# Level 0's odd maps: the high part held twice, one column apart, and level 2's stride-2 layer multiplied image by image

## The chip, the core and the metric

The kernel runs on one core of a Trainium2 chip. The metric is the device time of one execution in microseconds, lower is better. All times below are of this one core.

## What is computed

Two images of 32 channels and 64 x 64 pixels are normalised per channel, go through a small residual U-net, and are added to its result:

```python
def basic_block(x, w1, w2, stride=1, ds=None):
    out = jax.nn.relu(conv3(x, w1, stride) * BN_S)
    out = conv3(out, w2, 1) * BN_S
    identity = conv1x1(x, ds, stride) * BN_S if ds is not None else x
    return jax.nn.relu(out + identity)
...
x = basic_block(x, e0b0c1, e0b0c2)                          # level 0: 64 x 64
x = basic_block(x, e0b1c1, e0b1c2)
f0 = x
x = basic_block(x, e1b0c1, e1b0c2, stride=2, ds=e1b0ds)     # level 1: 32 x 32
x = basic_block(x, e1b1c1, e1b1c2)
f1 = x
x = basic_block(x, e2b0c1, e2b0c2, stride=2, ds=e2b0ds)     # level 2: 16 x 16
x = basic_block(x, e2b1c1, e2b1c2)
x = (jax.nn.relu(deconv2(x, dec0w) * BN_S) + f1) * BN_S
x = (jax.nn.relu(deconv2(x, dec1w) * BN_S) + f0) * BN_S
...
x = x + _L0_conv_ref(_gn(x), ...)
```

## The kernel before

**Maps in blocks.** A map of 64 x 64 pixels is kept as 32 x 32 blocks of 2 x 2 pixels: 4 pixels of a block times 32 channels fill the 128 partitions. A 3 x 3 convolution is then a sum over four shifts of a 2 x 2 stencil of blocks, each one product with a 128 x 128 weight. The output of the first convolution of a block pair lies half a block off, in 33 x 33 blocks (an "odd" map); the second convolution reads that map and returns to 32 x 32 ("even"). The four shifts `s` are (sy, sx) with sx = s mod 2.

**High and low parts.** Every operand is kept as an fp32r high part and an fp32r remainder. A piece of output is the sum of three groups of four matmuls: high weight by high map, low weight by high map, high weight by low map, 12 in all, into one PSUM bank.

**Stages and pieces.** The stages of level 0 are e0b0c1 (odd), e0b0c2 (even), e0b1c1 (odd), e0b1c2 (even). An odd stage has, per image, three pieces of 11 rows of 33 (364 columns a matmul, read as one run from the map `flat0`, pitch 33). An even stage has two pieces of 16 rows of 32 (512 columns) per image, read from the odd map `odd0`, laid out at L184 with `ODD0_PITCH` 36: `moving` (L948) takes 16 rows of 32 elements out of rows that are 36 apart. Pieces 0 to 5 are e0b0c1, 6 to 9 e0b0c2, 10 to 15 e0b1c1, 16 to 19 e0b1c2. Then come e1b0c1 (stride 2) and the rest of level 1 with 290 or 272 columns, level 2 with 164 or 144 for both images together, and the two upsampling stages.

**Who does what.** TensorE runs all matmuls in program order; nearly all are recorded on L837, the helper `products`. For an odd piece of level 0, VectorE applies ReLU and mask from the bank to `relu` (L763); ScalarE copies that to the high part (L545) and then prepares the high part of the next weight (`weights_hi`, L504); GpSimd subtracts to get the low part (L470). VectorE makes the low part of a weight (`weights_lo`, L604) after each piece; it needs `weights_hi` of the same weight, which ScalarE issues behind the high part of the piece before. VectorE writes a `relu` slot again only when the low part of four pieces earlier is there (L717). For an even piece VectorE adds the residual into `block0` (L767, L769), ScalarE makes the high part (L545, or L541 in e0b1c2) and VectorE the low part (L798, L793). SyncE loads the raw weights in four slots, each when the low part of the weight four earlier is done (L425).

**Level 2's stride-2 layer (e2b0c1).** Its input is split by pixel into four planes for both images. TensorE takes, for each image as it becomes ready, the five high products (L972, 82 columns); then for both images together five products of the low weights with the high map, five with the low map (L837, 164 columns), and, after waiting for `sides_by_act` and `sides_by_dve`, six with gathered half-width operands ("sides"). VectorE produces image 1's planes (L727, L734) behind its copies of sides for image 0 (L682); ScalarE gathers sides (L517) and, for the 1 x 1 shortcut, corners (L509), in the order sides of image 0, corners of image 0, sides of image 1, one corner of image 1. The next stage, e2b0c2, starts with three shortcut products once all corners are there (`corner_by_dve`, `corner_ready`), two filling matmuls on zeros, and 12 products of 144 columns that wait for e2b0c1's result from VectorE (L763).

**Skips.** ScalarE scales `block0` into `normed` (L554), GpSimd adds the input (L480), ScalarE reorders it into the tensor `skip0` (L578, 16 copies), for the last stage's additions.

Of the kernel before, what the change touches and what calls it, by code (L numbers as in the profile page):

```python
# [27 lines left out]
F32 = mybir.dt.float32  # L28
F32R = mybir.dt.float32r
BF16 = mybir.dt.bfloat16  # L30
ACT = mybir.ActivationFunctionType
ALU = mybir.AluOpType
# [8 lines left out]
ODD0_PITCH = 36  # L41
# [123 lines left out]
def build(nc, x, consts, weights, out):  # L165
    ctx = ExitStack()
    with ctx:  # L167
# [10 lines left out]
        skip0 = sb("skip0", [P, 8, IMAGES, 2, 8, 8])  # L178
# [5 lines left out]
        odd0 = sb("odd0", [P, 2, IMAGES, ODD_ROWS[0], ODD0_PITCH], F32R)  # L184
        flat1 = odd0[:].rearrange("p h i r c -> p (h i r c)")[:, 0:2 * IMAGES * MAP[1]].rearrange(
# [14 lines left out]
        odd = [odd0[:, :, :, :, 0:ODD_COLS[0]], odd1, odd2[:]]  # L200
# [160 lines left out]
        def split_of(piece, half):  # L361

            stage = STAGES[piece.stage]
            if stage.level == 0:
                if stage.kind == "odd":
                    return odd[0][:, half, piece.images[0], piece.row:piece.row + piece.rows, :]
                return flat_inside(half, piece.images, piece.row, piece.rows)
            return odd[stage.level][:, half] if stage.level == 2 else odd[1][:, half, piece.images[0]]
# [11 lines left out]
        def skip0_of(n):  # L380
            return skip0[:, n].rearrange("p i j a b -> p (i j a b)")

# [59 lines left out]
        def _(pool):  # L442
# [24 lines left out]
            for piece in LEVEL0:  # L467
                if STAGES[piece.stage].residual is None:
                    wait_half(pool, piece.index, 0)
                    pool.tensor_tensor(split_of(piece, 1), fp32_of(piece), split_of(piece, 0).bitcast(F32),  # L470
                                       ALU.subtract).then_inc(lo_ready, 1)
# [28 lines left out]
        def _(act):  # L500
# [36 lines left out]
            for piece in LEVEL0:  # L537
                wait_relu(act, piece.index)
                if STAGES[piece.stage].name == "e0b1c2":
                    for i in range(2):  # L540
                        last = act.activation(planes_inside(1, 0, piece.images[0], i, piece.row // 2, piece.rows // 2),  # L541
                                              fp32_of(piece)[:, i::2].rearrange("p r (c b) -> p b r c", b=2), ACT.Relu)
                    last.then_inc(hi_ready, 1)
                else:
                    act.activation(split_of(piece, 0), fp32_of(piece), ACT.Relu).then_inc(hi_ready, 1)  # L545
# [21 lines left out]
            gather_corners(2, 0)  # L567
            gather_sides(2, 1)
            gather_corners(2, 1, range(3, 4))
            for image in range(IMAGES):  # L570
                act.wait_ge(skip0_added, image + 1)
# [261 lines left out]
        def _(pe):  # L833
# [60 lines left out]
            for piece in PIECES[:DEC0[0].index]:  # L894
# [14 lines left out]
                elif level == 0:  # L909
                    target = rows_0(target, piece)  # L910
# [27 lines left out]

                def moving(half, s):
# [7 lines left out]
                    if level == 0:  # L947
                        return odd[0][:, half, images[0], piece.row + sy:piece.row + sy + piece.rows,  # L948
                                      sx:sx + BLOCKS[0]]
# [15 lines left out]
                if stage.kind == "down":  # L965

                    whole = [[moving(half, shifts * sy + sx) for sy, sx in WHOLE] for half in range(2)]
                    if level == 2:
                        for image in images:
                            wait_half(pe, source_of_level(2, image), 0)  # L970
                            for n, m in enumerate(whole[0]):
                                pe.matmul(target[:, image], w[:, 0, n], m[:, image], start=(image == 0 and n == 0),  # L972
                                          stop=False, skip_group_check=True)
                        wait_w_lo(pe, k)
                        products(target, [(w[:, 1, n], m) for n, m in enumerate(whole[0])], first=False, final=False,
                                 skip=True)
# [37 lines left out]
                last = products(target, low_terms, first=False, final=not shortcut_last)  # L1014
# [129 lines left out]
```

## Time and profile before

| | us |
|---|---|
| median of 3 runs | 91.69 (91.61 to 91.88) |
| the profiled execution | 91.54 |
| its span, first to last instruction | 89.7 |
| TensorE (PE) busy, share of the span | 83.0, 92% |
| VectorE (DVE) busy | 63.7, 71% |
| ScalarE (ACT) busy | 44.9, 50% |
| GpSimd (POOL) busy | 27.5, 31% |
| mean granted TensorE clock | 0.982 |

Busy shares say how full an engine is over the whole span, not whether it sets the end; for that one follows the chain of work that ended last, and in a stretch where one engine is on that chain, the distance from the start of one of its instructions to the start of the next. Matmuls overlap, so the duration recorded for one (some 400 ns for 512 columns) is longer than the time it takes in a stream; starts are what counts. PEld is the weight load that goes with each matmul.

### The profile page before, as it was taken

Reading aid. Unit: us, or ns where it says so; the run is one execution under the profiler, and the core shown is the slowest. Engines: PE = TensorE matmul, PEld = TensorE weight load, DVE = VectorE, ACT = ScalarE, POOL = GpSimd, SP = SyncE. Lnnn points to the kernel's source line nnn. Section 1 sums busy time; section 2 is a strip of 40 time slices with the busy share of each in tenths; the row PEclk is TensorE's granted clock in tenths of the full one; section 3 lists DMA queues with packets and bytes.
Section 4 is the critical chain, followed back from the end, with each engine's and each line's share of the span. In section 5 each row is a group of like instructions: output and inputs, shape, how many; then the busy total and the mean of one; then the engine's idle time right before and its main releaser. Section 6 shows DMA issues by size and latency. Waiting matters only on the chain.

```text
span 89.7 us, 1547 instructions
## 1 busy us (share of the span) xinstructions
PE 83.0 (92%) x537; PEld 73.9 (82%) x537; DVE 63.7 (71%) x189; ACT 44.9 (50%) x94; POOL 27.5 (31%) x43
## 2 busy tenths in 40 slices
PE   5988999999999999999999999999999989999900
PEld 3666999998777799999977777999999989887600
DVE  5579999799968799655635569999638797543650
ACT  6007015877435065744423259999910089990410
POOL 7300070999910000654440000300794002400140
PEclk9999999999999999999999999999999999999975
DMA  2989900045673003550000000000000000000075
GB/s 23 255 251 324 323 22 0 7 122 125 154 217 112 4 14 121 168 168 5 0 0 0 0 0 4 0 0 0 7 0 0 4 0 0 7 0 0 0 258 210
DMA packets 4183, 6.51 MB, mean 73 GB/s; under 512 B 464, under 2 KB 2128, under 8 KB 4176
## 3 DMA queue, kind: packets, MB, share of 16 engines
q1 hardware_dynamic: 4032, 6.29, 23.0%
q10 hardware_dynamic: 144, 0.13, 0.4%
q8 instruction: 4, 0.07, 0.3%
q14 instruction: 3, 0.02, 0.1%
HBM read 5.37 MB, written 1.05 MB: 72 GB/s over the span
## 4 chain that ended last, share of the span: by engine, by line
PE 83%; DVE 7%; DMA 3%; issue 1%; ACT 1%; POOLq 1%; DVEq 0%
PE psum L837 78%; DMA x_sb<-x_in 3%; PE psum L876 2%; DVE stats L611 2%; DVE split L727 1%; PE psum L972 1%; POOLq L167 1%; DVE shared L682 1%; PE psum L1029 1%; DVE split L734 1%; PE psum L862 1%; DVE moments L626 1%; DVE shared L640 1%; PE psum L869 1%; ACT result L586 0%
## 5 line engine op out<-in xcount | busy, mean ns | idle before, releaser
L470 POOL TENSOR_TENSOR odd<-relu,odd 128x363 fp32r<-128x363 f32 x12 | 13.4, 1134 | 16.0 <-ACT odd L545 16.0
L837 PE MATMUL psum<-shared,w_e0b0c 128*128 128x364 f32 x72 | 12.5, 332 | 0.4 <-DVE shared L640 0.4
L837 PEld LDWEIGHTS psum<-shared,w_e0b0c 128*128 128x128 f32 x72 | 12.0, 189 | 0.7 <-issue 0.7
L837 PE MATMUL psum<-shared,w_e0b1c 128*128 128x364 f32 x72 | 12.2, 329 | 0.0
L837 PEld LDWEIGHTS psum<-shared,w_e0b1c 128*128 128x128 f32 x72 | 12.1, 188 | 0.1
L837 PE MATMUL psum<-odd,w_e0b1c 128*128 128x512 f32 x48 | 12.0, 411 | 0.0
L837 PE MATMUL psum<-odd,w_e0b0c 128*128 128x512 f32 x48 | 12.0, 411 | 0.0
L763 DVE SCALAR_TENSOR_TENSOR relu<-psum,inside 128x363 f32<-128x363 f32 (+2 forms) x18 | 8.7, 489 | 3.8 <-PE psum L837 3.6
L837 PEld LDWEIGHTS psum<-odd,w_e0b0c 128*128 128x128 f32 x48 | 9.1, 190 | 2.6
L837 PEld LDWEIGHTS psum<-odd,w_e0b1c 128*128 128x128 f32 x48 | 9.1, 190 | 2.6
L545 ACT ACTIVATE odd<-relu 128x363 fp32r<-128x363 f32 x12 | 6.2, 520 | 7.4 <-DVE relu L763 7.4
L869 PE MATMUL psum<-zeros 128*128 128x256 bf16 x42 | 7.2, 330 | 1.1 <-DVE eps L660 1.1
L517 ACT ACTIVATE shared<-split 64x164 fp32r<-64x164 f32 (+2 forms) x7 | 3.1, 440 | 7.5 <-DVE split L734 6.5
L480 POOL TENSOR_TENSOR normed<-normed,x_sb 128x1024 f32<-128x1024 f32 x2 | 4.8, 2408 | 6.4 <-DVE shared L782 6.4
L869 PEld LDWEIGHTS psum<-zeros 128*128 128x128 bf16 x42 | 4.6, 119 | 2.4 <-DVE eps L660 1.1
L463 POOL TENSOR_TENSOR shared<-normed,shared 128x352 fp32r<-128x352 f32 (+1 forms) x4 | 3.2, 819 | 10.9 <-DVE normed L620 10.9
L545 ACT ACTIVATE shared<-block 128x512 fp32r<-128x512 f32 x4 | 2.5, 636 | 6.7 <-DVE block L767 6.7
L541 ACT ACTIVATE split<-block 128x256 fp32r<-128x256 f32 x8 | 3.0, 427 | 4.9 <-DVE block L769 4.8
L509 ACT ACTIVATE shared<-split 32x544 fp32r<-32x544 f32 x8 | 5.2, 656 | 0.1
L578 ACT ACTIVATE skip<-normed 128x128 f32<-128x128 f32 x16 | 5.2, 421 | 0.0
L837 PE MATMUL psum<-shared,w_e1b0c 128*128 128x272 f32 (+1 forms) x36 | 5.2, 292 | 0.0
L769 DVE SCALAR_TENSOR_TENSOR block<-block,psum 128x512 f32<-128x512 f32 x4 | 2.8, 689 | 3.0 <-PE psum L837 2.9
(126 smaller groups left out, 140.4 us busy)
## 6 DMA issues: line engine op xcount, KB each, us to landing
x_sb<-x_in SPq DMA_DIRECT2D x4, 160.0 KB, 3.9
raw<-e0b0c_in SPq DMA_DIRECT2D x2, 256.0 KB, 4.7
raw<-e0b1c_in SPq DMA_DIRECT2D x2, 256.0 KB, 4.9
raw<-e1b1c_in SPq DMA_DIRECT2D x2, 256.0 KB, 3.2
raw<-e2b1c_in SPq DMA_DIRECT2D x2, 256.0 KB, 2.6
raw<-e1b0c_in SPq DMA_DIRECT2D x1, 448.0 KB, 3.6
raw<-e2b0c_in SPq DMA_DIRECT2D x1, 448.0 KB, 4.1
x_sb<-x_in SPq DMA_DIRECT2D x2, 192.0 KB, 3.9
```

What stands on the lines that cost most here:

```text
L463: pool.tensor_tensor(flat_inside(1, [image], row, rows), normed[:, image, row:row + rows, :], flat_inside(0, [image], row, rows).bitcast(F32),
L470: pool.tensor_tensor(split_of(piece, 1), fp32_of(piece), split_of(piece, 0).bitcast(F32), ALU.subtract).then_inc(lo_ready, 1)
L480: pool.tensor_tensor(normed[:, image], normed[:, image], x_sb[:, image], ALU.add).then_inc(skip0_added, 1)
L509: last = act.activation(*corner_copy(level, image, q), ACT.Copy)
L517: last = act.activation(target, source, ACT.Copy)
L541: last = act.activation(planes_inside(1, 0, piece.images[0], i, piece.row // 2, piece.rows // 2), fp32_of(piece)[:, i::2].rearrange("p r ( ...
L545: act.activation(split_of(piece, 0), fp32_of(piece), ACT.Relu).then_inc(hi_ready, 1)
L578: last = act.activation(target, source, ACT.Copy)
L763: last = dve.scalar_tensor_tensor(out=target, in0=sums, scalar=0.0, in1=mask, op0=ALU.max, op1=ALU.mult)
L769: last = dve.scalar_tensor_tensor(out=target, in0=block0[:, image, rows, :], scalar=0.0, in1=sums, op0=ALU.max, op1=ALU.add)
L837: last = pe.matmul(target, w, moving, start=(first and n == 0), stop=(final and n == len(terms) - 1), skip_group_check=skip)
L869: pe.matmul(psum[:, bank, 0:256], zeros[:, 0:P], zeros[:, 0:256], start=True, stop=True)
```

## The change

The odd map of level 0 is split in two tensors. `odd0_hi` has no padding: rows of 32, and for each image two versions, version sx holding columns sx to sx + 31 of the 33. A shift's 16 rows are then one run of 512 elements. `odd0_lo` holds the low part once, with rows of 33 (before: 36), so its reads are still 16 rows of 32. ScalarE writes both versions (two activations of 32 columns a row where there was one of 33), and GpSimd subtracts in two steps, 32 columns against version 0 and the last column against version 1. `skip0` has no memory of its own any more and lies in `block0`, with a wait on ScalarE ahead of the first write. At level 2 the five low-weight products of e2b0c1 are made image by image, right behind the high ones, and ScalarE's corner copies of image 0 are split around its side copies of image 1.

```diff
 FLAT = (BLOCKS[0] + 2) * FLAT_PITCH + 2
-ODD0_PITCH = 36
 PITCH = [b + 1 for b in BLOCKS]
...
         block0 = sb("block0", [P, IMAGES, 32, 32])
-        skip0 = sb("skip0", [P, 8, IMAGES, 2, 8, 8])
+        skip0 = block0[:].rearrange("p i r c -> p (i r c)").rearrange("p (n i j a b) -> p n i j a b", n=8, i=IMAGES,
+                                                                     j=2, a=8)
         skip1 = sb("skip1", [P, 2, 2, 2, IMAGES, 8, 8], F32R)
...
         planes = [None, split0, split1]
-        odd0 = sb("odd0", [P, 2, IMAGES, ODD_ROWS[0], ODD0_PITCH], F32R)
-        flat1 = odd0[:].rearrange("p h i r c -> p (h i r c)")[:, 0:2 * IMAGES * MAP[1]].rearrange(
+        odd0_hi = sb("odd0_hi", [P, IMAGES, 2, ODD_ROWS[0], BLOCKS[0]], F32R)
+        odd0_lo = sb("odd0_lo", [P, IMAGES, ODD_ROWS[0], ODD_COLS[0]], F32R)
+        flat1 = odd0_hi[:].rearrange("p i v r c -> p (i v r c)")[:, 0:2 * IMAGES * MAP[1]].rearrange(
             "p (h i n) -> p h i n", h=2, i=IMAGES)
...
             "p (h i n) -> p h i n", h=2, i=IMAGES)
-        odd = [odd0[:, :, :, :, 0:ODD_COLS[0]], odd1, odd2[:]]
+        odd = [None, odd1, odd2[:]]
         corner = [None, corner1, corner2[:]]
...
             if stage.level == 0:
-                if stage.kind == "odd":
-                    return odd[0][:, half, piece.images[0], piece.row:piece.row + piece.rows, :]
                 return flat_inside(half, piece.images, piece.row, piece.rows)
...
             return skip0[:, n].rearrange("p i j a b -> p (i j a b)")
+
+        def high_shifted(piece, shift):
+            return odd0_hi[:, piece.images[0], shift, piece.row:piece.row + piece.rows, :]
+
+        def low_rows(piece):
+            return odd0_lo[:, piece.images[0], piece.row:piece.row + piece.rows, :]

...
                     wait_half(pool, piece.index, 0)
-                    pool.tensor_tensor(split_of(piece, 1), fp32_of(piece), split_of(piece, 0).bitcast(F32),
+                    last_column = slice(BLOCKS[0], ODD_COLS[0])
+                    pool.tensor_tensor(low_rows(piece)[:, :, 0:BLOCKS[0]], fp32_of(piece)[:, :, 0:BLOCKS[0]],
+                                       high_shifted(piece, 0).bitcast(F32), ALU.subtract)
+                    pool.tensor_tensor(low_rows(piece)[:, :, last_column], fp32_of(piece)[:, :, last_column],
+                                       high_shifted(piece, 1)[:, :, BLOCKS[0] - 1:].bitcast(F32),
                                        ALU.subtract).then_inc(lo_ready, 1)
...
                     last.then_inc(hi_ready, 1)
+                elif STAGES[piece.stage].kind == "odd":
+                    for shift in range(2):
+                        last = act.activation(high_shifted(piece, shift),
+                                              fp32_of(piece)[:, :, shift:shift + BLOCKS[0]], ACT.Relu)
+                    last.then_inc(hi_ready, 1)
                 else:
...
             gather_sides(2, 0)
-            gather_corners(2, 0)
+            gather_corners(2, 0, range(2))
             gather_sides(2, 1)
+            gather_corners(2, 0, range(2, 4))
             gather_corners(2, 1, range(3, 4))
             for image in range(IMAGES):
+                if image == 0:
+                    act.wait_ge(skip0_scaled, IMAGES)
                 act.wait_ge(skip0_added, image + 1)
...
                     target = bank_of(piece)[:, 0:flat_columns]
-                elif level == 0:
-                    target = rows_0(target, piece)

...

+                def summed_like(moved):
+                    return rows_0(target, piece) if len(moved.shape) == 3 and level == 0 else target
+
                 def moving(half, s):
...
                     if level == 0:
-                        return odd[0][:, half, images[0], piece.row + sy:piece.row + sy + piece.rows,
-                                      sx:sx + BLOCKS[0]]
+                        rows = slice(piece.row + sy, piece.row + sy + piece.rows)
+                        if half:
+                            return odd0_lo[:, images[0], rows, sx:sx + BLOCKS[0]]
+                        return odd0_hi[:, images[0], sx, rows, :].rearrange("p r c -> p (r c)")
                     source, run = (odd, EVEN_RUN) if stage.kind == "even" else (flat, RUN)
...
                             wait_half(pe, source_of_level(2, image), 0)
-                            for n, m in enumerate(whole[0]):
-                                pe.matmul(target[:, image], w[:, 0, n], m[:, image], start=(image == 0 and n == 0),
-                                          stop=False, skip_group_check=True)
-                        wait_w_lo(pe, k)
-                        products(target, [(w[:, 1, n], m) for n, m in enumerate(whole[0])], first=False, final=False,
-                                 skip=True)
+                            wait_w_lo(pe, k)
+                            for part in range(2):
+                                for n, m in enumerate(whole[0]):
+                                    pe.matmul(target[:, image], w[:, part, n], m[:, image],
+                                              start=(image == 0 and part == 0 and n == 0),
+                                              stop=False, skip_group_check=True)
                     else:
...
                 wait_source(piece, 1)
-                last = products(target, low_terms, first=False, final=not shortcut_last)
+                last = products(summed_like(low_terms[0][1]), low_terms, first=False, final=not shortcut_last)
                 if shortcut_last:
```

## Rows read from the trace of the kernel before

**Rows 1.** Page, section 4: the chain that ended last, by line:

```profile
PE psum L837 78%; DMA x_sb<-x_in 3%; PE psum L876 2%; DVE stats L611 2%; DVE split L727 1%; PE psum L972 1%; POOLq L167 1%; DVE shared L682 1%; PE psum L1029 1%; DVE split L734 1%; PE psum L862 1%; DVE moments L626 1%; DVE shared L640 1%; PE psum L869 1%; ACT result L586 0%
```

**Rows 2.** TensorE by stretch, last three stages of level 0: length, busy (count), granted clock, DMA:

```profile
20.39:32.20 11.81, 11.81 (x49) 1.00 0.43 114
32.20:44.25 12.05, 12.05 (x74) 1.00 0.29 88
44.25:56.06 11.81, 11.81 (x50) 1.00 0.00 1
```

**Rows 3.** TensorE timeline: start, us, engine, line, operation, operands; level 1:

```profile
65.57 3.37 PE L837 MATMUL psum<-odd,w_e1b1c 128*128 128x290 f32 x24
68.78 0.41 PE L837 MATMUL psum<-odd,eye_r 128*128 128x272 f32 x2
69.03 1.68 PE L837 MATMUL psum<-shared,w_e1b1c 128*128 128x272 f32 x12
70.55 0.42 PE L837 MATMUL psum<-odd,eye_r 128*128 128x272 f32 x2
```

**Rows 4.** TensorE timeline, narrow windows in e0b0c2; the first start in each counts:

```profile
20.88 0.66 PE L837 MATMUL psum<-odd,w_e0b0c 128*128 128x512 f32 x2
21.12 0.65 PE L837 MATMUL psum<-odd,w_e0b0c 128*128 128x512 f32 x2
21.37 0.66 PE L837 MATMUL psum<-odd,w_e0b0c 128*128 128x512 f32 x2
21.61 0.66 PE L837 MATMUL psum<-odd,w_e0b0c 128*128 128x512 f32 x2
```

**Rows 5.** Groups by line and form: busy us, mean ns of one; idle before, releaser:

```profile
L545 ACT ACTIVATE odd<-relu 128x363 fp32r<-128x363 f32 x12 | 6.2, 520 | 7.4 <-DVE relu L763 7.4
L496 POOL TENSOR_TENSOR result<-result,skip 128x256 f32<-128x256 f32 x2 | 1.5, 726 | 7.8 <-ACT result L586 7.8
```

**Rows 6.** Timeline of all engines, e0b0c1, e0b0c2 and the start of e0b1c2:

```profile
15.93 0.52 ACT L545 ACTIVATE odd<-relu 128x363 fp32r<-128x363 f32 x1 [0.82 <-DVE relu L763]
16.35 0.61 ACT L504 ACTIVATE w_e0b0c<-raw 128x512 fp32r<-128x512 f32 x1
17.07 7.92 POOL L470 TENSOR_TENSOR odd<-relu,odd 128x363 fp32r<-128x363 f32 x6
30.37 0.69 DVE L798 SCALAR_TENSOR_TENSOR shared<-block,shared 128x512 fp32r<-128x512 f32 x1
45.61 0.91 POOL L470 TENSOR_TENSOR odd<-relu,odd 128x363 fp32r<-128x363 f32 x1 [1.08 <-ACT odd L545]
```

**Rows 7.** Timeline of all engines, level 2, e2b0c1:

```profile
72.31 0.65 PE L972 MATMUL psum<-split,w_e2b0c 128*128 128x82 f32 x5
73.25 0.75 PE L972 MATMUL psum<-split,w_e2b0c 128*128 128x82 f32 x5 [0.29 <-DVE split L727]
73.83 1.33 PE L837 MATMUL psum<-split,w_e2b0c 128*128 128x164 f32 x10
73.89 0.99 DVE L682 CAST shared<-split 32x164 fp32r<-32x164 f32 x4
74.35 0.69 ACT L517 ACTIVATE shared<-split 64x164 fp32r<-64x164 f32 x2
74.91 0.70 DVE L812 CAST corner<-split 32x144 fp32r<-32x144 f32 x3
75.09 0.90 PE L837 MATMUL psum<-shared,w_e2b0c 128*128 128x164 f32 x6
75.87 0.53 PE L837 MATMUL psum<-corner,w_e2b0ds 128*128 128x144 f32 x3
76.03 0.33 DVE L763 SCALAR_TENSOR_TENSOR odd<-psum,inside 128x164 fp32r<-128x164 f32 x1 [0.42 <-PE psum L837]
76.42 1.56 PE L837 MATMUL psum<-odd,w_e2b0c 128*128 128x144 f32 x12
```

**Rows 8.** TensorE timeline, one narrow window late in e2b0c1:

```profile
74.89 0.27 PE L837 MATMUL psum<-split,w_e2b0c 128*128 128x164 f32 x1
```

## The prediction

> **What bounds the kernel now.** I began with the chain of work that ended last [rows 1]: TensorE's matmuls on L837 alone are 78% of the span; no line of another engine has over 3%. So I read TensorE first and the other engines only where they release it. The stretches of level 0 [rows 2] show it without a gap: 11.81, 12.05 and 11.81 us, busy for the whole length, at a granted clock of 1.00, which is the upper level, 2.4 GHz. There a microsecond is won only by making matmuls start closer together.
>
> How close are they? An even stage of level 0 has 4 pieces of 12 matmuls of 512 columns: 11.81 us over 48 is 246 ns each, 0.48 ns a column. An odd stage has 72 of 364 columns: 12.05 us over 72 is 167.4 ns, 0.46 ns a column [rows 2]. In level 1, 24 matmuls of 290 columns take 65.57 to 68.78, 133.8 ns each, and 12 of 272 take 69.03 to 70.55, 126.7 ns: 0.461 and 0.466 ns a column [rows 3]. All of these but the 512s read one unbroken run. A straight line through the three unbroken sizes has a slope of about 0.45 ns a column and puts 512 at 233 ns. If only the clock's 0.417 ns were added for each column above 364 it would be 229, and at a fixed 0.46 a column 235.5. So broken reads cost some 10 to 17 ns a matmul.
>
> A second look says why. Within e0b0c2 the starts are 20.88, 21.12, 21.37 and 21.61 [rows 4]: 0.24, 0.25, 0.24. The starts of all 48 matmuls of the stage, of which these are four, alternate that way to the end, with means of 242 ns after shifts with sx = 0 and 250.5 ns after sx = 1, and the last stage gives the same two means. A row pitch of 36 elements is 144 bytes, so every row begins on a multiple of 16 bytes for sx = 0 and 4 bytes past one for sx = 1; no other difference between the shifts alternates like that. Start alignment of the 16 rows thus costs 8.5 ns, and the row breaks another 242 - 233 = 9 ns.
>
> **Part 1, the high map in one run.** Of the 12 matmuls of an even piece, 8 read the high map (high and low weight, four shifts each). Two stages with 4 pieces each make 8 x 8 = 64 matmuls. They go from 246 to 233 ns: 64 x 13.2 = 0.84 us less, all on the path that sets the end. The bounds are 64 x 10.5 = 0.67 (235.5 ns) and 64 x 17 = 1.09 (229 ns) within this mechanism; outside it, see the rivals. I take 233 because it lies between the two extrapolations and uses three sizes.
>
> Here a rule of the Trainium skill speaks against a part of the gain. The rows show that alignment matters and that aligned rows of 32 take 242 ns [rows 4]. The page "SBUF — State Buffer", in the note on cachelines in the section "Door 1: The DMA port swizzle", says that SBUF has 16-byte lines and that each step to a new line has a price. 16 aligned rows touch as many lines as one aligned run of 512, so by that rule alone the run would take 242 ns and not 233. That is rival A.
>
> **Part 2, the low map at pitch 33.** The other 4 matmuls a piece, 32 in all, still read 16 rows of 32, now 33 apart. The start of a row moves by one element from row to row: a quarter of the rows starts on a multiple of 16 bytes with either sx, where before it was all with sx = 0 and none with sx = 1, half on average. With 8.5 ns for sixteen unaligned rows the mean goes from 246 to 248.4 ns: 32 x 2.1 = +0.07 us. Bounds: 0, and 32 x 4.3 = 0.14 if all rows counted as unaligned.
>
> **Part 3, the extra work of ScalarE and GpSimd in level 0.** ScalarE now makes two activations of 352 elements for one of 363; one is 0.52 us [rows 5], and the next instruction starts 0.42 us after it, at 16.35 behind 15.93 [rows 6]. That is 0.42 us more for each of 12 pieces, 5 us of an engine that is at 50%. GpSimd gets a second subtraction of 11 elements. No row has one so small. The upper bound is the 0.73 us of a two-input operation of 256 elements [rows 5], the lower is 0; the line through that and 0.91 us for 363 [rows 6] leaves 0.3 us at 11 elements, which I take. Everything else the edit moves on ScalarE's queue is the preparation of the next weight (L504), and VectorE's low weight (L604) and its next ReLU queue behind that; SyncE's next load waits for the low weight. I replayed these queues. The high part of piece 1 is ready at 18.1 instead of 17.4; TensorE wants it at 20.39, the start of the stage [rows 2]. VectorE falls behind by up to 1.5 us about piece 5, since each of its low weights waits for ScalarE. GpSimd's six subtractions of the first odd stage, 17.07 to 24.99 [rows 6], end near 27; the last low part is wanted by the fourth even piece, after 28.9 + 8 x 0.23 = 30.8. The tightest later place is the low part of piece 7 (L798), done at 30.37 + 0.69 = 31.06 [rows 6] and now at some 32.4, wanted by the ninth matmul of piece 11 at about 35. In the second odd stage a piece lasts 2.0 us and ScalarE needs 0.84 + 0.6. So the price is 0, hidden under TensorE's stream with 2 us to spare; were that cover gone, the whole lag of up to 1.5 us would be TensorE's. Below nothing it can't go: nothing on TensorE waits for these engines there now.
>
> The `skip0` wait and its place in `block0` cost nothing: the scaling it waits for is over some 10 us earlier on the same engine.
>
> **Part 4, e2b0c1 by image.** Before, TensorE does five matmuls at 72.31, idles for 0.29 us for image 1's planes, and starts again at 73.25. From there 15 matmuls follow, the last at 74.89, and the six on sides start at 75.09 [rows 7, 8]. Five of 82 columns take 73.25 to 73.83, 0.116 us each; the ten of 164 have nine intervals from 73.83 to 74.89, 0.118 each [rows 7, 8], of which all but the first are at 0.1125. At these sizes the width doesn't matter, only the count. The edit therefore adds five matmuls (31 for 26), 5 x 0.11 = 0.56 us. Placed behind image 0's high products they fill the idle time: ten matmuls from 72.31 end at 73.33 + 0.03, a loss of 0.08 to 0.1 against 73.25. From there again 15 matmuls (ten for image 1, five low) at 0.1125: the sides could start at 75.02. Before, that start was held up by ScalarE, whose two side copies of image 1 ended at 74.35 + 0.69 = 75.04, as they stood behind the corner copies [rows 7]. In the new order they start when image 1's low planes are there, 73.9, and end near 74.6; VectorE's copies are next late, 73.89 + 0.99 = 74.88, just under. The wait seems to cost the matmuls right behind it something too: the six sides take 75.09 to 75.87, 0.13 each [rows 7]. Without the wait, six at 0.1125 bring the next start to 75.70. VectorE's corners are done at 75.61, so the shortcut products don't wait. The result on VectorE (76.03) and the next matmuls (76.42) come 0.17 us earlier. I take 0.17 us less; bounds: 0.1 us more (nothing recovered but the later start), and 0.25 less. Behind it TensorE, VectorE and ScalarE hand over to one another to the end, so this passes on whole.
>
> **The sum.** -0.84 + 0.07 + 0 - 0.17 = -0.94 us. The profiled execution took 91.54 us (span 89.7 and 1.84 around it), so the changed one should take 90.60. The median of the runs was 91.69, 0.15 above the profiled one: 90.75.
>
> **Rivals.** A, alignment only: the row breaks are free, the line through three sizes doesn't reach to 512, and both copies merely run at the 242 ns that sx = 0 has now. 64 x 4.2 = 0.27; with the other parts -0.37: 91.32. For it: the 242 is measured, 233 is extrapolated. Against it: 242 is 0.473 ns a column, more than at any unbroken size.
>
> B, nothing in level 0: the two means come from something other than where rows begin, say the order of weights, and 512 columns cost 246 anyway. 0.07 - 0.17: 91.59. The alternation with sx in both even stages speaks against it.
>
> C, the run goes at full clock. By rows, that would be 512 columns at 0.417 ns, 213 ns, and nothing in between: 64 x 33 = 2.1 us less, 89.5 with the rest. Against it: 364 unbroken columns should then take 152 ns and take 167. The Trainium skill, "TensorE: Matmul & The Clock Gate", "Back-to-back issue gap", gives columns over 2.4 GHz and 2.5 ns; the trace disagrees by 13 ns at 364.
>
> D, slower: ScalarE's second copy makes TensorE wait. The place is the start of e0b0c2 at 20.39, for the high part of piece 1. The replay leaves 2.3 us there. It decides once ScalarE's path is later than that; to end slower by over 0.3% it must also eat the 0.94 us and 0.28 more, so the high part must come at about 21.6, 3.5 us later than replayed. The time would be 92.0. Only port conflicts or a far slower activation could do it; L545 is steady at 520 ns [rows 5].
>
> **How the numbers follow.** Forecast 0.55, A 0.17, B 0.10, C 0.06, D 0.05, and 0.07 for mixtures. The forecast's own range, with 0.67 to 1.09, 0 to 0.14, and +0.1 to -0.25, is 90.4 to 91.25. A lies just beyond, at 91.32, and the range takes it in: 90.3 to 91.4. Outside are B, C, D and some of the mixtures, 0.2 or a little more. A difference of about 0.3% (0.28 us) is what a measurement of this kernel can tell from no change. Faster than 91.41: the forecast, C, most of A, and part of the mixtures, 0.77; the same: the rest of A, B, 0.16; slower: D and the worst mixtures, 0.07.
>
> **What would show it.** In the profile after: e0b0c2 and e0b1c2 each last 11.81 - 0.39 = 11.4 us; within a piece, eight starts 0.23 apart with no alternation and four 0.25 apart. Eight at 0.24 is rival A, at 0.246 B. In e2b0c1 no idle time ahead of image 1, the sides about 75.0 less the gain before it, and e2b0c2's 12 matmuls some 0.17 us nearer to the end of e1b1c2. If TensorE is idle anywhere from e0b0c2 to e1b0c1, D is at work. The prediction is wrong if a flat run is not what makes the 364-column matmuls cheap per column, or if VectorE's or ScalarE's pieces of e2b0c1 shift.

## The result, and the profile after

| | before | changed |
|---|---|---|
| median of 19 runs, us | 91.76 | 92.02 |
| ratio, 95% interval | | 1.0031 (1.0017 to 1.0045) |
| the profiled execution, us | 91.54 | 91.98 |
| its span | 89.7 | 90.2 |
| TensorE busy | 83.0 | 82.9 |
| ScalarE busy | 44.9 | 49.1 |
| GpSimd busy | 27.5 | 30.3 |

All times compared are of undisturbed executions; the only trace of one later run, e5, is of a disturbed execution (granted clock 0.645) and is not read. The changed kernel is slower by 0.3%, where 1.0% less was forecast. Yet the part that was meant to gain did gain. TensorE by stretch in the changed kernel, the same three stages as in [rows 2] (length, busy and count, granted clock, DMA):

```profile
20.57:31.80 11.23, 11.23 (x50) 1.00 0.43 134
31.80:43.83 12.03, 12.03 (x74) 1.00 0.31 89
43.83:55.06 11.23, 11.23 (x50) 1.00 0.00 0
```

Each even stage takes 11.23 us for 11.81: 1.16 us less for the two. So the reader must look for 1.4 us elsewhere. Cutting both executions at the same places of the program gives it, in us:

| stretch | before | changed | difference |
|---|---|---|---|
| start to the first product of e0b0c1 | 8.02 | 8.25 | +0.23 |
| e0b0c1 and e0b1c1 | 24.42 | 24.35 | -0.07 |
| e0b0c2 and e0b1c2 | 23.62 | 22.46 | -1.16 |
| start of e1b0c1 to the sides of its image 1 | 4.86 | 5.30 | +0.44 |
| from there to e2b0c1 | 11.39 | 11.45 | +0.06 |
| e2b0c1 to e2b0c2's 12 products | 4.11 | 4.10 | -0.01 |
| from there to the end of GpSimd's last addition | 10.11 | 10.09 | -0.02 |
| from there to the end of the span | 3.2 | 4.2 | +1.0 |

The first line isn't the change's. In the profiled executions of the experiments below the first product starts anywhere from 7.94 to 8.55 us, with the level 0 part (8.06 in e1 and e4, 8.53 in e9) as well as without it (8.02 in e3, 8.30 in e2, 8.55 in e6). Why it varies wasn't looked into. Two later lines are the change's: 0.44 us at the start of level 1 and 1.0 us after all engines are done. With -1.16 they make +0.28, and the medians differ by 0.26.

**Where level 1 loses.** Timeline of the kernel before, last pieces of e0b1c2 and start of e1b0c1 (start, us, engine, line, operation):

```profile
53.32 0.69 DVE L769 SCALAR_TENSOR_TENSOR block<-block,psum 128x512 f32<-128x512 f32 x1 [0.56 <-PE psum L837]
55.94 0.94 DVE L682 CAST shared<-split 32x580 fp32r<-32x580 f32 x2
56.91 0.69 DVE L769 SCALAR_TENSOR_TENSOR block<-block,psum 128x512 f32<-128x512 f32 x1
59.48 1.29 DVE L697 CAST shared<-split 32x308 fp32r<-32x308 f32 x4
60.92 0.37 PE L837 MATMUL psum<-shared,w_e1b0c 128*128 128x290 f32 x1
```

and the same stretch of the changed kernel:

```profile
52.45 0.69 DVE L786 SCALAR_TENSOR_TENSOR block<-block,psum 128x512 f32<-128x512 f32 x1 [0.41 <-PE psum L854]
54.28 0.90 DVE L810 SCALAR_TENSOR_TENSOR split<-block,split 128x128 fp32r<-128x128 f32 x4 [0.19 <-ACT split L550]
55.22 1.10 DVE L699 CAST shared<-split 32x580 fp32r<-32x580 f32 x2
55.28 0.16 POOL L456 MEMSET odd_hi<- 128x72 f32 x1 [8.65 <-PE psum L854]
56.35 0.69 DVE L786 SCALAR_TENSOR_TENSOR block<-block,psum 128x512 f32<-128x512 f32 x1
58.10 2.25 PE L854 MATMUL psum<-split,w_e1b0c 128*128 128x290 f32 x15
58.92 1.29 DVE L714 CAST shared<-split 32x308 fp32r<-32x308 f32 x4
60.36 2.56 PE L854 MATMUL psum<-shared,w_e1b0c 128*128 128x290 f32 x18
```

VectorE works without a break from the block addition of piece 18 (53.32, 52.45) to the last side copy (ended 60.77, 60.21); but for 0.19 us in the changed kernel, where it waits for ScalarE. TensorE starts on the sides 0.15 us after that copy in both kernels (60.92, 60.36), also in the changed one, where it waits for them. So the 0.15 us is the handover, and not time in hand: before, VectorE was ready just when TensorE came, with nothing to spare (TensorE's start there, 60.92, is 0.16 us behind the one before it, where its stream otherwise goes at 0.13 to 0.14). A shorter e0b1c2 brings TensorE there earlier but not VectorE's and ScalarE's work, and that work grew by 0.3 us: 0.19 waiting for ScalarE and 0.16 in the side copies. TensorE loses the 0.44 us in two halves: 0.21 before the first products of image 1 (58.10) and 0.23 before its sides (60.36).

**Where the end loses.** Both kernels in half-microsecond stretches, the columns being length, then busy time of PE, PEld, DVE, ACT and POOL, granted clock, share of the DMA engines, GB/s. Before:

```profile
88.00:88.50 0.50, 0.00 (x0) 0.00 (x0) 0.00 (x0) 0.00 (x0) 0.00 (x0) 0.50 1.00 399
88.50:89.00 0.50, 0.00 (x0) 0.00 (x0) 0.00 (x0) 0.00 (x0) 0.00 (x0) 0.50 0.32 123
89.00:89.50 0.50, 0.00 (x0) 0.00 (x0) 0.00 (x0) 0.00 (x0) 0.00 (x0) 0.50 0.00 0
```

and changed:

```profile
87.50:88.00 0.50, 0.00 (x0) 0.00 (x0) 0.00 (x0) 0.00 (x0) 0.00 (x0) 1.00 0.95 381
88.00:88.50 0.50, 0.00 (x0) 0.00 (x0) 0.00 (x0) 0.00 (x0) 0.00 (x0) 0.65 0.24 92
88.50:89.00 0.50, 0.00 (x0) 0.00 (x0) 0.00 (x0) 0.00 (x0) 0.00 (x0) 0.50 0.08 31
89.00:89.50 0.50, 0.00 (x0) 0.00 (x0) 0.00 (x0) 0.00 (x0) 0.00 (x0) 0.50 0.03 12
```

The bulk of the stores is done 0.5 us earlier than before, but a share of 0.08 and then 0.03 goes on for a microsecond: about one of the 16 DMA engines (0.06) has its part left. The last store lands 3.7 us after its issue instead of 2.7. Queues in the last 6 us, before (queue, kind: packets, MB, share; q1 and q10 carry the stores, q14 instructions):

```profile
q1 hardware_dynamic: 576, 0.92, 41.7%
q10 hardware_dynamic: 144, 0.13, 6.6%
```

and in 87 to 88 us of the changed kernel:

```profile
q1 hardware_dynamic: 150, 0.38, 96.4%
q14 instruction: 1, 0.01, 7.7%
```

One packet of instructions, of 8 KB (the expectations below put it at 7), is fetched there. 7.7% of 16 engines for 1 us is 1.23 us of one DMA engine: the packet starts at 87.18 and ends at 88.41. What the queues still have from 88.35 us to the end:

```profile
q1 hardware_dynamic: 9, 0.02, 5.8%
```

These nine are eight packets of 3 KB, one behind another every 0.12 us from 88.40 on, and a closing one of 4 bytes. 384 KB over 16 engines is eight such packets for each, so this is one engine's whole part of the last store, and it begins when the instruction packet ends; the others' parts were over at 88.28. What brought the packet there, and whether the loss goes when it goes, is what the experiments asked.

### The profile page after: what moved, and what is told of

Read it like the earlier page. It is cut to its first block, busy times and chain, and to the rows that moved or that the text cites. A ratio compares the mean times of both kernels' runs of the same rounds, so it can differ in the third digit from the quotient of the medians.

```text
span 90.2 us, 1584 instructions
## 1 busy us (share of the span) xinstructions
PE 82.9 (92%) x542; PEld 74.7 (83%) x542; DVE 65.0 (72%) x189; ACT 49.1 (54%) x106; POOL 30.3 (34%) x55
## 4 chain that ended last, share of the span: by engine, by line
PE 90%; DVE 2%; ACT 1%; POOLq 1%; issue 1%
PE psum L854 77%; PE psum L886 6%; PE psum L893 2%; PE psum L994 2%; POOLq L166 1%; PE psum L1049 1%; PE psum L879 1%; DVE moments L643 1%; DVE shared L657 1%; ACT shared L600 0%; ACT result L603 0%; DVE flat L765 0%; DVE scratch L652 0%; DVE scratch L647 0%; DVE scratch L648 0%
## 5 line engine op out<-in xcount | busy, mean ns | idle before, releaser
L476 POOL TENSOR_TENSOR odd_lo<-relu,odd_hi 128x352 fp32r<-128x352 f32 x12 | 10.6, 886 | 13.1 <-ACT odd_hi L555 13.1
L555 ACT ACTIVATE odd_hi<-relu 128x352 fp32r<-128x352 f32 x24 | 10.6, 489 | 4.2 <-DVE relu L780 4.1
L886 PE MATMUL psum<-zeros 128*128 128x256 bf16 x42 | 7.8, 353 | 1.1 <-DVE eps L677 1.1
L854 PE MATMUL psum<-odd_hi,w_e0b0c 128*128 128x512 f32 x32 | 8.1, 394 | 0.0
L854 PE MATMUL psum<-odd_hi,w_e0b1c 128*128 128x512 f32 x32 | 8.1, 394 | 0.0
L854 PEld LDWEIGHTS psum<-odd_hi,w_e0b1c 128*128 128x128 f32 x32 | 6.0, 188 | 1.4
L854 PEld LDWEIGHTS psum<-odd_hi,w_e0b0c 128*128 128x128 f32 x32 | 6.0, 188 | 1.4
L478 POOL TENSOR_TENSOR odd_lo<-relu,odd_hi 128x11 fp32r<-128x11 f32 x12 | 6.4, 532 | 0.0
L595 ACT ACTIVATE block<-normed 128x128 f32<-128x128 f32 x16 | 5.2, 436 | 0.0
```

The costliest lines, as they stand in the source:

```text
L476: pool.tensor_tensor(low_rows(piece)[:, :, 0:BLOCKS[0]], fp32_of(piece)[:, :, 0:BLOCKS[0]], high_shifted(piece, 0).bitcast(F32), ALU.subtract)
L478: pool.tensor_tensor(low_rows(piece)[:, :, last_column], fp32_of(piece)[:, :, last_column], high_shifted(piece, 1)[:, :, BLOCKS[0] - 1:].b ...
L555: last = act.activation(high_shifted(piece, shift), fp32_of(piece)[:, :, shift:shift + BLOCKS[0]], ACT.Relu)
L595: last = act.activation(target, source, ACT.Copy)
L854: last = pe.matmul(target, w, moving, start=(first and n == 0), stop=(final and n == len(terms) - 1), skip_group_check=skip)
L886: pe.matmul(psum[:, bank, 0:256], zeros[:, 0:P], zeros[:, 0:256], start=True, stop=True)
```

## The experiments

**First four: which part, and is it the place in memory?** The parts of the change, one at a time. e1 is the changed kernel with:

```diff
-        skip0 = block0[:].rearrange(...)
+        skip0 = sb("skip0", [P, 8, IMAGES, 2, 8, 8])
...
-                if image == 0:
-                    act.wait_ge(skip0_scaled, IMAGES)
```

> The changed kernel, but skip0 has memory of its own again and its wait is gone, so that result and all tensors behind it up to odd0 lie at the addresses of the kernel before. In the changed kernel's profile the last engine instruction ends 0.53 us earlier than before, yet the span is 0.5 us longer: from the last instruction to the end of the span it takes 4.2 us for 3.2, and the last store lands 3.7 us after its issue for 2.7. Theory P (place): the store's last us comes from where skip0 and result lie. Then here it lands in 2.7 us, and the kernel takes 91.98 - 1.0 = 91.0, some 0.8% less than before. Theory I (instructions): it comes with the longer instruction streams (1584 for 1547, a fourth packet in an instruction queue). Then nothing changes against the changed kernel: 1.003 of before, 3.7 us. Both expect level 1 to begin 1.0 us earlier than before and to lose 0.4 to 0.5 us before e1b0c2.

Measured: 91.93 us against 91.81 for the kernel before, run beside it, 1.0012 (0.9993 to 1.0031); the last store landed 3.7 us after its issue, and q14 had its fourth packet at the end. The place in memory is not it.

e2 is the kernel before with the reverse of that edit:

```diff
-        skip0 = sb("skip0", [P, 8, IMAGES, 2, 8, 8])
+        skip0 = block0[:].rearrange(...)
...
+                if image == 0:
+                    act.wait_ge(skip0_scaled, IMAGES)
```

> The kernel before with skip0 in block0 and the wait for it, nothing else. Theory P: about 1 us slower than before (1.010), all of it after the last engine instruction. Theory I: the same as before within 0.2 us, since one wait is all that is added.

Measured: 91.76 against 91.81, 1.0001 (0.9982 to 1.0020), last store 2.7 us. Theory P has fallen, and `skip0` in `block0` costs nothing, as predicted.

e3 is the kernel before with the level 2 part:

```diff
                         for image in images:
                             wait_half(pe, source_of_level(2, image), 0)
-                            for n, m in enumerate(whole[0]):
-                                pe.matmul(target[:, image], w[:, 0, n], ...)
-                        wait_w_lo(pe, k)
-                        products(target, [(w[:, 1, n], m) for n, m in enumerate(whole[0])], ...)
+                            wait_w_lo(pe, k)
+                            for part in range(2):
+                                for n, m in enumerate(whole[0]):
+                                    pe.matmul(target[:, image], w[:, part, n], ...)
...
-            gather_corners(2, 0)
+            gather_corners(2, 0, range(2))
             gather_sides(2, 1)
+            gather_corners(2, 0, range(2, 4))
```

> The kernel before with the level 2 part alone (low-weight products by image, corner copies split). The prediction's step: 0.17 us less from the start of e2b0c1 to e2b0c2's 12 matmuls. The changed kernel's trace shows 4.10 us there for 4.11, so the theory after the fact: nothing, 1.000 within 0.1 us, since the shortcut products wait for VectorE's last corner copy, which the edit doesn't move. Theory I expects up to 1 us more if the five added matmuls carry TensorE's stream over a limit; theory P expects none.

Measured: 91.62 against 91.81, 0.9982 (0.9960 to 1.0005). In its trace e2b0c1 begins at 72.24 and e2b0c2's 12 products at 76.31, 4.07 us for 4.11; the store lands after 2.8 us. At most 0.04 us of the 0.17 came; the interval holds both. Five more instructions on TensorE bring no packet.

e4 is the kernel before with the level 0 part alone, reads and writes as in the change:

```diff
-        odd0 = sb("odd0", [P, 2, IMAGES, ODD_ROWS[0], ODD0_PITCH], F32R)
+        odd0_hi = sb("odd0_hi", [P, IMAGES, 2, ODD_ROWS[0], BLOCKS[0]], F32R)
+        odd0_lo = sb("odd0_lo", [P, IMAGES, ODD_ROWS[0], ODD_COLS[0]], F32R)
...
```

> The kernel before with the level 0 part alone (high map twice, low map at pitch 33), skip0 in memory of its own. The prediction gave this part -0.77 us. By the changed kernel's trace: two even stages at 11.23 for 11.81 us, 1.16 less, of which level 1 loses 0.45, so -0.7 us, 0.992 of before, under theory P. Under theory I the store's us comes on top (12 more activations on ScalarE, 12 more operations on GpSimd): 1.003.

Measured: 91.92 against 91.81, 1.0014 (0.9994 to 1.0034), store 3.7 us, fourth packet of q14. The level 0 part alone does everything: gain, loss at level 1 and loss at the end.

**Next four: whose instructions?** The level 0 part adds 12 instructions on ScalarE and 12 on GpSimd. e5 takes ScalarE's away again:

```diff
-                    for shift in range(2):
-                        last = act.activation(high_shifted(piece, shift),
-                                              fp32_of(piece)[:, :, shift:shift + BLOCKS[0]], ACT.Relu)
-                    last.then_inc(hi_ready, 1)
+                    rows = fp32_of(piece)[:, :, 0:BLOCKS[0]]
+                    both = type(rows)(rows.tensor, rows.offset, [rows.ap[0], [1, 2]] + list(rows.ap[1:]))
+                    act.activation(odd0_hi[:, piece.images[0], :, piece.row:piece.row + piece.rows, :], both,
+                                   ACT.Relu).then_inc(hi_ready, 1)
```

> The changed kernel, but ScalarE writes both versions of the high map in one activation of 704 elements (the source read twice, a column apart): 12 instructions fewer on ScalarE, as many as before the change. In the profiles so far the last store lands 3.7 us after its issue exactly where a fourth 7 KB packet of instruction queue q14 lies in the last 6 us (the changed kernel, e1, e4), and 2.7 us where q14 has three packets, none of them there (before, e2, e3). Theory A (ScalarE's stream is fetched by q14 and its length puts the last fetch into the stores): back to 2.7 us, 1.0 us less than the changed kernel, about 91.0, 0.992 of before. Theory G (GpSimd's stream does it, which keeps its 12 more): 3.7 us, 1.003 of before.

Measured: 91.99 against 91.76, 1.0010 (0.9984 to 1.0036). Theory A wanted 0.992, which the interval excludes. The store is read in e8, which contains the same edit: 3.8 us after its issue, with the packet. Not ScalarE.

e6 and e7 go the other way and pad the kernel before.

```diff
+        pad = sb("pad", [P, 12])
...
+                    if STAGES[piece.stage].kind == "odd":
+                        act.activation(pad[:, ...], eps4[:, 0:1], ACT.Copy)
```

> The kernel before with 12 one-element activations more on ScalarE, one after each high part of an odd piece, whose results nobody reads. Theory A: q14 gets a fourth packet during the stores, the last store lands 3.7 us after its issue, 1.0 us slower (1.011). Theory G: no difference beyond 0.1 us.

```diff
...
+                    slot = piece.index % 10 + 6 * (piece.index >= 10)
+                    pool.memset(pad[:, slot:slot + 1], 0.0)
```

> The kernel before with 12 one-element memsets more on GpSimd, one after each low part of an odd piece, whose results nobody reads. Theory G: fourth q14 packet during the stores, last store 3.7 us after its issue, 1.0 us slower (1.011). Theory A: no difference beyond 0.1 us.

Measured: e6 91.87 against 91.76, 1.0006 (0.9984 to 1.0027), store 2.7 us, no packet in the last 6 us. e7 92.69 (four runs), 1.0095 (1.0061 to 1.0130), store 3.7 us. The queues of e7 from 84 us to its end:

```profile
q1 hardware_dynamic: 576, 0.92, 35.2%
q10 hardware_dynamic: 144, 0.13, 5.6%
q14 instruction: 1, 0.01, 1.1%
```

Twelve memsets of one element, on an engine that is idle two thirds of the time and whose results nobody reads, cost the kernel before 0.9 us. It is GpSimd's instruction stream that brings the packet. And it is the packet that holds the store up: in e1, e4, e7 and e8 too, eight packets of 3 KB follow one another on one engine to the end, and the first starts within 0.01 us of the instruction packet's end (at 88.17, 88.23, 89.31 and 88.39 us).

e8 adds to e5 a later clearing of borders on GpSimd:

```diff
-            pool.wait_ge(summed, last_piece(STAGE["e0b1c2"], range(IMAGES), BLOCKS[0] - 1) + 1)
+            pool.wait_ge(summed, last_piece(STAGE["e1b0c1"], range(IMAGES), 0) + 1)
             ground(flat1.bitcast(F32).rearrange("p h i n -> p (h i) n"), 1)
```

> e5 with one thing more: GpSimd clears the borders of flat1 after e1b0c1's second piece instead of after the last piece of e0b1c2. In the changed kernel these memsets (55.28 to 56.0) run beside VectorE's two side copies of image 0, which take 1.10 us for 0.94 before the change, where the memsets came later. Theory of contention: the copies take 0.94 us again, VectorE's block addition of the last piece starts 0.16 us earlier relative to the end of e0b1c2, and the kernel is 0.1 to 0.16 us faster than e5. Rival: the copies are long for another reason; no difference to e5.

Measured: 1.0014 (0.9989 to 1.0039), which can't tell 0.16 us. The trace can, VectorE in e8:

```profile
55.35 0.93 DVE L699 CAST shared<-split 32x580 fp32r<-32x580 f32 x2
56.31 0.69 DVE L786 SCALAR_TENSOR_TENSOR block<-block,psum 128x512 f32<-128x512 f32 x1
```

The copies take 0.93 us again instead of 1.10, and from the end of e0b1c2 (55.20) to the sides of image 1 (60.33) it is 5.13 us for 5.30. GpSimd's memsets beside them were what stretched the copies: e8's other edit, e5's, acts on ScalarE a stage earlier.

**Last four: can the loss be taken back?** If it is the moment of the fetch and not its existence, still more instructions should help. e9 is the changed kernel with 12 more memsets on GpSimd:

```diff
...
+                    slot = 1 * (piece.index % 10 + 6 * (piece.index >= 10))
+                    for more in range(1):
+                        pool.memset(pad[:, slot + more:slot + more + 1], 0.0)
                     pool.tensor_tensor(low_rows(piece)[:, :, last_column], ...)
```

> The changed kernel with 12 one-element memsets more on GpSimd (one between the two subtractions of each odd piece; nobody reads them), so 72 instructions there for 60 and for 48 before the change. Theory G2 (what costs is not the number of fetches but that GpSimd's last one falls into the stores; more instructions ahead of it bring it forward): q14's packet leaves the last 6 us, the last store lands 2.7 us after its issue, and the kernel is 1.0 us faster than the changed one, 91.0, 0.992 of before. Rival G1 (each further packet at the end costs, however many): 3.7 us or more, 1.003 or slower.

Measured: 90.97 against 91.68, 0.9927 (0.9900 to 0.9954), store 2.8 us, and no instruction packet in the last 6 us: q14's 8 KB packets start at 26.0, 41.9, 62.6 and 71.0 us, where the changed kernel had 25.8, 41.6, 70.6 and 87.2. The same number of memsets that made the kernel before 0.95% slower makes the changed one about 1.0% faster (0.9927 against 1.0031). With -1.16 and +0.44 left, the sum says -0.72 us; measured is -0.71.

e10 is e9, with e8's later clearing, and the last two side copies of image 0 given to GpSimd as soon as their source is there:

```diff
+            pool.wait_ge(lo_ready, 12)
+            wait_half(pool, LEVEL0[-3].index, 1)
+            for n, copy in enumerate(SIDES[4:6]):
+                pool.tensor_copy(*side_copy(1, 0, copy)).then_inc(sides_by_pool, 1)
+                pool.wait_ge(sides_by_pool, n + 1)
...
-                if piece is LEVEL0[-2]:
-                    side_copies(1, 0, 4, 2)
...
+                    if level == 1 and images[-1] == 0:
+                        pe.wait_ge(sides_by_pool, 2)
```

> e9, and GpSimd takes the last two side copies of image 0 at level 1 off VectorE (two waits added on GpSimd, one on TensorE) and clears flat1's borders later. Theory of the chain: in the changed kernel level 1 loses 0.44 us, since from the third piece of e0b1c2 on, VectorE's and ScalarE's work to the sides of image 1 takes 7.7 us, and a shorter stage doesn't shorten it. Two copies less on VectorE (0.94 to 1.10 us) make it shorter than TensorE's own path, so e1b0c1's image 1 starts and its sides start without a gap: the 5.30 us from the end of e0b1c2 to those sides become 4.86, 0.44 us less than e9, 90.6, 0.987 of before. Rival: GpSimd's copies of 32 partitions are slow or keep VectorE from its port, and the gain is lost or turned: 0 to 0.3 us slower than e9.

Measured: 90.63 (five runs) against 91.68, 0.9885 (0.9854 to 0.9917). Its TensorE at the start of level 1:

```profile
54.78 2.18 PE L862 MATMUL psum<-split,w_e1b0c 128*128 128x290 f32 x15
56.80 0.96 PE L862 MATMUL psum<-shared,w_e1b0c 128*128 128x290 f32 x6
57.61 2.21 PE L862 MATMUL psum<-split,w_e1b0c 128*128 128x290 f32 x15
59.71 2.55 PE L862 MATMUL psum<-shared,w_e1b0c 128*128 128x290 f32 x18
```

54.78 to 59.71 is 4.93 us, against 5.30 in the changed kernel and 4.86 before. The loss at level 1, but for 0.07 us, was VectorE's load there.

e11 is the kernel before with e10's copies and clearing.

> The kernel before with e10's rearrangement of copies and borders alone. There the same chain ended 0.2 us ahead of TensorE, so the theory of the chain expects nothing from level 1 (1.000 within 0.15 us), unless the two instructions more on GpSimd move its last fetch into the stores, which would show as 1.0 us more.

Measured: 91.61 against 91.68, 0.9988 (0.9961 to 1.0016), 4.83 us for 4.86. Before the change those copies were free.

e12 is e10 without the 12 memsets, and so a kernel with no useless work in it.

> e10 without its 12 memsets: 62 instructions and three waits more on GpSimd than the changed kernel's 60. By theory G2 all depends on where GpSimd's last fetch falls: with 60 it lay in the stores, with 72 and 74 it didn't. Two more are few against the 112 that a 7 KB packet holds at 64 bytes each, so I expect it still in the stores: last store 3.7 us, level 1 as good as in e10 (4.9 us to the sides), 1.0 us slower than e10: 91.65, 0.999 of before. If the fetch has moved out, 90.6, 0.988.

Measured: 90.82 against 91.73, 0.9901 (0.9869 to 0.9932). My expectation of 91.65 missed. The packet is there, but elsewhere. Queues of e12 from 85 to 86 us:

```profile
q1 hardware_dynamic: 241, 0.22, 65.2%
q10 hardware_dynamic: 84, 0.09, 25.6%
q14 instruction: 1, 0.01, 3.1%
```

It starts at 85.00, 1.0 us after the first store was issued, and takes 3.1% of 16 engines for 1 us, 0.50 us of one engine, not 1.23; the last store lands after 2.7 us. So being among the stores isn't enough. The last store, issued at 85.83, finds the packet already done (85.50). In the changed kernel, e1, e4, e7 and e8 the packet starts 1.1 to 1.3 us after the last store's issue. That its place against the last store decides is read from these traces; it wasn't varied by itself. Two copies and a few waits on GpSimd were enough to move it.

## Why the prediction was wrong, step by step

**Part 1 (high map in one run): right in mechanism and size.** In e0b0c2 the first eight matmuls go from 20.57 to 22.42, timeline of the changed kernel:

```profile
20.57 2.02 PE L854 MATMUL psum<-odd_hi,w_e0b0c 128*128 128x512 f32 x8
22.42 1.11 PE L854 MATMUL psum<-odd_lo,w_e0b0c 128*128 128x512 f32 x4
23.37 2.01 PE L854 MATMUL psum<-odd_hi,w_e0b0c 128*128 128x512 f32 x8
```

The mean of all 64 is 231.8 ns, where 233 was forecast and 229 and 235.5 were the bounds, and the alternation with sx is gone. The same 64 took 246.6 ns before, so they save 0.95 us (forecast 0.84). The prediction read the two alternating means slightly wrong: by all starts of the two stages they are 241.1 and 251.0 ns, not 242 and 250.5; nothing hangs on that. Rival A would have given 242 ns, and so would the rule of the Trainium skill, "SBUF — State Buffer", note on cachelines in "Door 1: The DMA port swizzle", as I applied it. This trace disagrees: the run is 9 ns faster than sixteen aligned rows (231.8 against 241.1), which touch as many 16-byte lines, so here the count of lines alone doesn't decide. Rival C's 213 ns didn't come either.

**Part 2 (low map at pitch 33): wrong sign.** The four low matmuls take 0.95 us in the first piece; the mean of all 32 is 238.4 ns. The forecast was 248.4, by starts of rows off a multiple of 16 bytes. The same 32 took 245.2 ns before, at pitch 36, so pitch 33 is 6.8 ns faster: -0.22 us, not +0.07. The inference from the alternation was too narrow: it showed that the place of a row matters at pitch 36 and was carried to another pitch. Rows that follow one another with a gap of one element cost 7 ns over an unbroken run, rows with a gap of four 9 to 19. Why wasn't tested. Level 0 thus gained 1.16 us, not 0.77, and the net result was worse all the same.

**Part 3 (ScalarE and GpSimd hidden): right where it looked.** No stage of level 0 waits: stages begin without a gap. Rival D, ScalarE late at the start of e0b0c2, didn't happen. ScalarE's busy time rose by 4.2 us (I took 5), hidden. GpSimd's second subtraction took 0.53 us on average where I took 0.3, also hidden. But the part priced GpSimd's 12 instructions only by engine time. Their price of 1.0 us lay in the instruction stream (e7, e9), which the profile before does show, as a queue of kind instruction, and which I didn't read. "So the price is 0" is the step that failed, and by the largest term.

**The gain "all on the path that sets the end": wrong.** Part 1 took every nanosecond of the even stages for the kernel's. It held for e0b0c2. For e0b1c2, I asked how far the engines behind TensorE lag, from the first odd stage to piece 11, and stopped there. What had to be asked as well is what comes due when TensorE arrives 0.58 us earlier at e1b0c1, and the timeline before shows VectorE with nothing in hand there: its last side copy ends one handover, 0.15 us, ahead of TensorE's start on the sides. Price 0.44 us; e8 and e10 show 0.17 of it as the border clearing and nearly all of it as VectorE's two copies and that clearing together.

**Part 4 (e2b0c1 by image): mostly wrong in effect, and small.** The step-by-step order held: image 1's planes cost no idle time, the sides begin 2.75 us after the start (forecast 2.71) and go at 0.11 us each. But the shortcut products begin no earlier: 75.39 in the changed kernel, 3.58 us after the start, before 3.56 [rows 7]. The sentence that failed is "VectorE's corners are done at 75.61, so the shortcut products don't wait". In the changed kernel they are done at 75.10 and TensorE's weight load starts at 75.36; before it was 75.61 and 75.83. TensorE had waited for them before as well, with 0.2 us from the copy's end to its start, and the edit moves nothing of that. Why this wait takes 0.2 us where the one on image 1's planes takes 0.05 (before, from 73.20 to 73.25) stays open.

**The sum.** Forecast -0.94: -0.84, +0.07, 0, -0.17. Found: -0.95, -0.22 (together 1.16 by the stages), +1.0 and +0.44 for the two that stood at nothing, -0.0 for level 2. Rival D had the side right, and TensorE does wait, but at level 1 and not for ScalarE's second copy at 20.39. None of the rivals had the fetch.

## What to carry to other kernels

When a stage is made faster, replay the other engines not only to where they lag today but to the next place where TensorE will arrive early; an engine that is ready there just when TensorE comes is the next bound. Read the instruction queues' packets with their times, before and after: an instruction added to an idle engine can cost more than anything it computes, if a fetch slides into the final stores, and here two copies and a few waits on that engine were enough to move it. Before judging an edit slow, split the difference by stretches of the program; here a gain of 1.16 us was hidden behind two losses elsewhere.

## What the hardware showed that I had not expected

- Twelve one-element memsets on GpSimd made one kernel 0.95% slower (1.0095) and, measured from the changed one at 1.0031, another about 1.0% faster (0.9927). ScalarE's twelve (e6) and TensorE's five (e3) did nothing.
- An instruction packet of 8 KB took 0.97 to 1.23 us of one DMA engine among the large packets of the last store (five traces), and that engine's part of the store began only behind it; it took 0.50 us at the start of the stores (e12), and 0.37 us alone (2.3% of 16 engines in 71 to 72 us of the kernel before).
- 512 columns of fp32r per matmul: 231.8 ns in one run, 238.4 in rows of 32 at pitch 33, 241.1 and 251.0 at pitch 36.
- The kernel that beats both, e12, has the whole change in it, with two copies given to GpSimd and the border clearing later: 0.9901 (0.9869 to 0.9932). e10, with the memsets, has 0.9885, and the two intervals overlap.
